# Three subtractions ahead of the multiplications in both normalizations of a post-norm transformer layer

## The chip, the cores and the metric

The kernel runs on one Trainium2 chip, on all 8 of its cores, as one program. The time is that of the device in microseconds, from start to end of the slowest core. No core talks to another: each computes 1024 token rows of the output.

## What is computed

```python
x = L0_attn_x                      # 4 x 2048 x 4096, float32
x = _layernorm(x + _L0_attn_ref(x, Wq, Wkv, Wo, bo))
x = _layernorm(x + _L0_ffn_ref(x, lora_A, lora_B, W, bias, lora_weights))

def _layernorm(x, axis=-1, eps=1e-5):
    m = jnp.mean(x, axis=axis, keepdims=True)
    v = jnp.var(x, axis=axis, keepdims=True)
    return (x - m) / jnp.sqrt(v + eps)
```

The attention has 32 heads of width 128 that share 8 groups of keys and values, with a causal mask. The second part is a product with a 4096 x 4096 matrix plus eight low-rank products of rank 16 that are summed.

## The kernel before, in words

A core holds its 1024 tokens along the free dimension; the 4096 features are 32 tiles of 128 partitions, indexed mc (or kc). So a tile of activations is 128 x 1024. The program is written engine by engine: each step appends a function to a list of its engine (em("v", ...) for VectorE, "t" TensorE, "c" ScalarE, "s" the SyncE queue, "g" the GpSimd queue), and each engine runs its list in the order written, with semaphores between them. There is no scheduler.

The stages are: keys and values for all tokens of the batch (L258, L269), queries (L336, L342), attention (L414 to L477), the division by the softmax sums (L526), the output projection with the first residual r1 (L585, L591, then L623/L625), which is stored to r1sc in DRAM, tile by tile, while two sums per token are collected on TensorE. f_v_fin1 makes mean and inverse deviation from the sums (L658 to L674); they go through DRAM (vec4) and come back broadcast to 128 partitions as bcm1 and bca1 (L682, L683).

**Stretch Y, the first normalization** (for mc in 0..31, f_v, L719 and L720): the tile r1[mc] is read back by SyncE (emit_r1rd, L542) into one of four slots, VectorE subtracts bcm1 into sb_y32 (L719) and multiplies that by bca1 into the bf16 tile ybf[mc] (L720). The helper vsync makes VectorE wait for the instruction it has just issued, and each tile waits for v_y of the one before. The read of tile mc, from 4 on, waits for v_y of tile mc-4. When all 32 are there, TensorE computes the low-rank product (f_t_h, L729, L735), then the big one (L765, L767); meanwhile r1 is read once more and normalized again, this time on VectorE with L794/L795, and the second residual r2 (L804, L806) is stored to r2sc (L824).

**Stretch O, the second normalization and the output**: after the second pair of sums (L830 to L846) SyncE loads the broadcast vectors bcm2 and bca2 (L854, L855) and the first four tiles of r2 (emit_r2rd, L870). Then per tile: VectorE subtracts (L886) and multiplies (L887) into one of two output buffers, SyncE stores it to the output (L892) and then reads tile mc+4. That order on SyncE is written as

```python
            def f_s2(sy, mc=mc):
                sy.wait_ge(SM["v_out"], mc + 1)
                sy.dma_start(out=d_out[mc], in_=vf32(OFF_OUTB[mc % 2], TOK)).then_inc(SM["so_out%d" % (mc % 2)], 16)
            em("s", f_s2)
            if mc + 4 < DC:
                emit_r2rd(mc + 4)
```

and is the same in both kernels. A subtraction waits for its read, for v_out of the tile before, and from tile 2 on for the store of tile mc-2 (so_out), which used the same output buffer.

Of the kernel before, what the change touches and what calls it, by code (L numbers as in the profile page):

```python
# [15 lines left out]
DC = 32  # L16
# [3 lines left out]
TOK = 1024  # L20
# [64 lines left out]
def build_nc():  # L85
# [38 lines left out]
    def sv(i):  # L124
        return arena[0:1, OFF_SV[i]:OFF_SV[i] + 4 * TOK].bitcast(F32)

    def ltmp(i):
        return arena[0:1, OFF_LTMP[i]:OFF_LTMP[i] + 4 * TOK].bitcast(F32)
    sb_r1bf = vbf(OFF_R1BF, TOK)
# [23 lines left out]
    def em(e, f):  # L153
        prog[e].append((cur_phase[0], f))
# [15 lines left out]
    with ExitStack() as es:  # L170
# [11 lines left out]
            "s_exp", "t_mmpc", "v_evl", "v_evctx", "v_norm", "v_nmul",  # L182
            "t_mmwo", "v_r1", "s_stats", "t_stats", "v_stat", "s_sqrt",
            "v_y", "t_mmh", "v_evh", "v_lbt", "t_mmf", "v_r2", "s_st2",
            "t_st2", "v_stat2", "s_sqrt2", "v_out", "v_seq",
        ]
        SM = {n: es.enter_context(nc.semaphore(n)) for n in semnames}

# [343 lines left out]
        def emit_r1rd(idx, extra_waits):  # L532
            slot = idx % 4
            r1rdc[slot] += 1
            tgt = 16 * r1rdc[slot]
            mc = idx % DC
            off = OFF_R1RD[slot]

            def f(sy, idx=idx, mc=mc, slot=slot, off=off, extra_waits=tuple(extra_waits)):
                for sn, val in extra_waits:  # L540
                    sy.wait_ge(SM[sn], val)
                sy.dma_start(out=vf32(off, TOK), in_=d_r1[mc]).then_inc(SM["sr1rd%d" % slot], 16)  # L542
            em("s", f)
            return tgt
# [159 lines left out]
        em("v", f_v_lbt)  # L704

        for mc in range(4, DC):
            r1rd_tgt[mc] = emit_r1rd(mc, [("v_y", mc - 3),
                                          ("ss_r1%d" % (mc % 2), 16 * (mc // 2 + 1))])
        for mc in range(DC):

            def f_v(v, mc=mc):
                slot = mc % 4
                v.wait_ge(SM["sr1rd%d" % slot], r1rd_tgt[mc])
                if mc == 0:
                    v.wait_ge(SM["s_bc"], 32)
                else:
                    v.wait_ge(SM["v_y"], mc)
                r1in = vf32(OFF_R1RD[slot], TOK)
                vsync(v, v.tensor_sub(sb_y32[:], r1in[:], sb_bcm1[:]))  # L719
                v.tensor_mul(sb_ybf[:, mc * TOK:(mc + 1) * TOK], sb_y32[:], sb_bca1[:]).then_inc(SM["v_y"], 1)  # L720
            em("v", f_v)

        def f_t_h(t):
            t.wait_ge(SM["s_lat"], 16)
# [24 lines left out]
        pending_stats2 = None  # L749
        for mc in range(DC):  # L750
            slot = mc % 2
            r1rd_tgt[DC + mc] = emit_r1rd(DC + mc, [("v_r2", mc - 3)] if mc >= 4 else [("v_y", DC)])

            def f_t(t, mc=mc, slot=slot):
                t.wait_ge(SM["gw%d" % slot], wt_tgt[mc])
                if mc == 0:
                    t.wait_ge(SM["v_evh"], 1)
                    t.wait_ge(SM["v_lbt"], 1)
                if mc >= 2:
                    t.wait_ge(SM["v_r2"], mc - 1)  # L760
                pair = P[mc % 2][:]
                wb = vbf(OFF_WBLK[slot], DC * 128)
                for kc in range(DC):
                    st = wb[:, kc * 128:(kc + 1) * 128]
                    t.matmul(pair[:, 0:512], st, sb_ybf[:, kc * TOK: kc * TOK + 512],  # L765
                             start=(kc == 0), stop=False)
                    t.matmul(pair[:, 512:1024], st, sb_ybf[:, kc * TOK + 512:(kc + 1) * TOK],  # L767
                             start=(kc == 0), stop=False)
                stl = sb_lbtb[:, mc * 128:(mc + 1) * 128]
                t.matmul(pair[:, 0:512], stl, sb_hb[:, 0:512], start=False, stop=True)  # L770
                t.matmul(pair[:, 512:1024], stl, sb_hb[:, 512:1024], start=False, stop=True).then_inc(SM["t_mmf"], 1)
            em("t", f_t)
            if pending_stats2 is not None:
                em("t", pending_stats2)

            def f_t_stats(t, mc=mc):
                t.wait_ge(SM["s_st2"], 2 * (mc + 1))
                if mc == 0:
                    t.wait_ge(SM["v_stat"], 2)
                t.matmul(P45[0:1, 0:512], sb_ones[:], sb_r1bf[:, 0:512],  # L780
                         start=(mc == 0), stop=(mc == DC - 1))
                t.matmul(P45[0:1, 512:1024], sb_ones[:], sb_r1bf[:, 512:1024],
                         start=(mc == 0), stop=(mc == DC - 1))
                t.matmul(P67[0:1, 0:512], sb_ones[:], sb_sqbf[:, 0:512],
                         start=(mc == 0), stop=(mc == DC - 1))
                t.matmul(P67[0:1, 512:1024], sb_ones[:], sb_sqbf[:, 512:1024],
                         start=(mc == 0), stop=(mc == DC - 1)).then_inc(SM["t_st2"], 1)

            def f_v(v, mc=mc, slot=slot):
                rslot = (DC + mc) % 4  # L790
                v.wait_ge(SM["sr1rd%d" % rslot], r1rd_tgt[DC + mc])
                if mc >= 1:
                    v.wait_ge(SM["v_r2"], mc)
                vsync(v, v.tensor_sub(sb_y32[:], vf32(OFF_R1RD[rslot], TOK)[:], sb_bcm1[:]))  # L794
                vsync(v, v.tensor_mul(sb_y32[:], sb_y32[:], sb_bca1[:]))  # L795
                v.wait_ge(SM["t_mmf"], mc + 1)
                if mc < 2:
                    v.wait_ge(SM["v_r1"], DC)
                if mc >= 2:
                    v.wait_ge(SM["ss_r2%d" % slot], 16 * (mc // 2))  # L800
                    v.wait_ge(SM["s_st2"], 2 * (mc - 1))
                pair = P[mc % 2][:]
                r2b = vf32(OFF_R2BUF[slot], TOK)
                v.scalar_tensor_tensor(r2b[:, 0:512], pair[:, 0:512], sb_bi[:, mc:mc + 1],  # L804
                                       sb_y32[:, 0:512], ALU.add, ALU.add)
                v.scalar_tensor_tensor(r2b[:, 512:1024], pair[:, 512:1024], sb_bi[:, mc:mc + 1],  # L806
                                       sb_y32[:, 512:1024], ALU.add, ALU.add).then_inc(SM["v_r2"], 1)
            em("v", f_v)

            def f_c(sc, mc=mc, slot=slot):  # L810
                sc.wait_ge(SM["v_r2"], mc + 1)
                if mc >= 1:
                    sc.wait_ge(SM["t_st2"], mc)
                if mc == 0:
                    sc.wait_ge(SM["t_stats"], DC)
                r2b = vf32(OFF_R2BUF[slot], TOK)
                sc.copy(sb_r1bf[:], r2b[:])  # L817
                sc.activation(sb_sqbf[:], r2b[:], AF.Square, bias=0.0, scale=1.0).then_inc(SM["s_st2"], 2)
            em("c", f_c)
            pending_stats2 = f_t_stats  # L820

            def f_s2(sy, mc=mc, slot=slot):
                sy.wait_ge(SM["v_r2"], mc + 1)
                sy.dma_start(out=d_r2[mc], in_=vf32(OFF_R2BUF[slot], TOK)).then_inc(SM["ss_r2%d" % slot], 16)  # L824
            em("s", f_s2)
# [35 lines left out]
        def emit_r2rd(mc):  # L861
            slot = mc % 4

            def f_s(sy, mc=mc, slot=slot):
                sy.wait_ge(SM["ss_r2%d" % (mc % 2)], 16 * (mc // 2 + 1))
                if slot >= 2 and mc < 4:
                    sy.wait_ge(SM["t_mmf"], DC)
                if mc >= 4:
                    sy.wait_ge(SM["v_out"], mc - 3)
                sy.dma_start(out=vf32(OFF_R2RD[slot], TOK), in_=d_r2[mc]).then_inc(SM["sr2rd%d" % slot], 16)  # L870
            em("s", f_s)

        for mc in range(4):
            emit_r2rd(mc)
        for mc in range(DC):
            slot = mc % 4

            def f_v(v, mc=mc, slot=slot):
                v.wait_ge(SM["sr2rd%d" % slot], r2rd_tgt6[mc])
                if mc == 0:  # L880
                    v.wait_ge(SM["s_bc"], 64)
                else:
                    v.wait_ge(SM["v_out"], mc)
                if mc >= 2:
                    v.wait_ge(SM["so_out%d" % (mc % 2)], 16 * (mc // 2))
                vsync(v, v.tensor_sub(sb_y32[:], vf32(OFF_R2RD[slot], TOK)[:], sb_bcm2[:]))  # L886
                v.tensor_mul(vf32(OFF_OUTB[mc % 2], TOK)[:], sb_y32[:], sb_bca2[:]).then_inc(SM["v_out"], 1)  # L887
            em("v", f_v)

            def f_s2(sy, mc=mc):  # L890
                sy.wait_ge(SM["v_out"], mc + 1)
# [4 lines that stand above are left out]
# [158 lines left out]
```

## Time and profile before

| what | us |
|---|---|
| median of 2 runs | 2995.86 |
| the runs | 2978.42 and 3013.3 |
| profiled execution, its own time | 2977.04 |
| its span on the slowest core (core 6) | 2975.4 |
| spans of the 8 cores | 2957.7 to 2975.4 |

The span is the time from the first to the last instruction of a core; the execution's own time lies 1.6 us above it. Rows of the trace are from core 6, in microseconds from the start of its span.

### The profile page before, as it was taken

Reading aid. Unit: us, or ns where it says so; the run is one execution under the profiler, and the core shown is the slowest. Engines: PE = TensorE matmul, PEld = TensorE weight load, DVE = VectorE, ACT = ScalarE, POOL = GpSimd, SP = SyncE. Lnnn points to the kernel's source line nnn. Section 1 sums busy time; section 2 is a strip of 40 time slices with the busy share of each in tenths; the row PEclk is TensorE's granted clock in tenths of the full one; section 3 lists DMA queues with packets and bytes.
Section 4 is the critical chain, followed back from the end, with each engine's and each line's share of the span. In section 5 each row is a group of like instructions: output and inputs, shape, how many; then the busy total and the mean of one; then the engine's idle time right before and its main releaser. Section 6 shows DMA issues by size and latency. Waiting matters only on the chain.

```text
span 2975.4 us, 32751 instructions; the slowest of 8 cores (2957.7 to 2975.4 us)
## 1 busy us (share of the span) xinstructions
PE 2441.4 (82%) x13257; PEld 1232.5 (41%) x13440; DVE 574.3 (19%) x662; ACT 551.8 (19%) x644; POOL 72.4 (2%) x140
## 2 busy tenths in 40 slices
PE   3888898899999878888988489999940799999900
PEld 3777787744444323333333134444410344444400
DVE  0110110100000001111111520000039222222256
ACT  0000000000000066677666111111110011111100
POOL 0000000000000000000000000000000000000000
PEclk9999998999999989999999689999975899999955
DMA  8878878544544410000000576666636455555558
GB/s 136 134 143 148 150 136 147 114 89 89 100 95 91 94 35 16 15 15 14 13 15 15 169 202 156 142 142 141 142 100 197 85 134 135 137 140 142 128 204 269
DMA packets 67129, 339.72 MB, mean 114 GB/s; under 512 B 8004, under 2 KB 8004, under 8 KB 49704
## 3 DMA queue, kind: packets, MB, share of 16 engines
q0 software_dynamic: 19584, 181.97, 35.1%
q1 hardware_dynamic: 47400, 155.65, 14.9%
q8 instruction: 111, 1.82, 0.2%
q14 instruction: 34, 0.28, 0.0%
HBM read 460.55 MB, written 59.00 MB: 175 GB/s over the span
## 4 chain that ended last, share of the span: by engine, by line
PE 75%; DMA 14%; DVE 8%; issue 2%; ACT 0%; DVEq 0%; SPq 0%; POOL 0%; POOLq 0%; ACTq 0%
PE P L767 8%; DMA arena<-xs 8%; PE P L342 7%; PE P L765 7%; PE P L591 7%; PE P L336 7%; PE P L585 7%; PE P L258 5%; PE P L269 5%; PE P L434 2%; PE P L443 2%; PE P L436 2%; DMA out<-arena 2%; PE P L448 2%; PE P L439 2%; PE P L445 2%
## 5 line engine op out<-in xcount | busy, mean ns | idle before, releaser
L477 ACT ACTIVATE arena<-P,arena 128x512 bf16<-128x512 f32 (+7 forms) x512 | 418.9, 830 | 183.9 <-PE P L414 145.8
L591 PE MATMUL P<-arena 128*128 128x512 bf16 x992 | 384.1, 387 | 24.6 <-DVE arena L526 21.4
L585 PE MATMUL P<-arena 128*128 128x512 bf16 x981 | 378.7, 386 | 21.3 <-DVE arena L526 21.3
L767 PE MATMUL P<-arena 128*128 128x512 bf16 x1024 | 389.3, 380 | 3.0 <-issue 1.0
L342 PE MATMUL P<-arena 128*128 128x512 bf16 x992 | 377.6, 381 | 12.1 <-DMA arena<-wq 10.0
L765 PE MATMUL P<-arena 128*128 128x512 bf16 x980 | 372.9, 381 | 11.5 <-DMA arena<-wt 11.5
L336 PE MATMUL P<-arena 128*128 128x512 bf16 x983 | 374.1, 381 | 0.0
L258 PE MATMUL P<-arena 128*128 128x256 bf16 x2048 | 247.0, 285 | 109.1 <-DMA arena<-xs 62.7
L258 PEld LDWEIGHTS P<-arena 128*128 128x128 bf16 x2048 | 207.5, 102 | 146.9 <-issue 114.7
L269 PE MATMUL P<-arena 128*128 128x256 bf16 x2048 | 228.8, 273 | 0.0
L269 PEld LDWEIGHTS P<-arena 128*128 128x128 bf16 x2048 | 200.4, 98 | 23.1
L477 ACT ACT_TABLE_LOAD x1 | 1.3, 1283 | 1050.0 <-PE P L414 1050.0
L585 PEld LDWEIGHTS P<-arena 128*128 128x128 bf16 x1024 | 100.4, 98 | 196.4 <-issue 83.2
L765 PEld LDWEIGHTS P<-arena 128*128 128x128 bf16 x1024 | 100.4, 98 | 143.1 <-issue 26.5
L336 PEld LDWEIGHTS P<-arena 128*128 128x128 bf16 x1024 | 100.6, 98 | 131.7 <-issue 11.8
L767 PEld LDWEIGHTS P<-arena 128*128 128x128 bf16 x1024 | 100.4, 98 | 117.9 <-issue 1.4
L342 PEld LDWEIGHTS P<-arena 128*128 128x128 bf16 x992 | 97.4, 98 | 117.9 <-issue 1.6
L463 DVE COPY arena<-P 1x1024 f32<-1x1024 f32 x32 | 38.8, 1212 | 548.0 <-PE P L448 548.0
L591 PEld LDWEIGHTS P<-arena 128*128 128x128 bf16 x992 | 97.3, 98 | 110.2 <-issue 0.5
L817 ACT CAST arena<-arena 128x1024 bf16<-128x1024 f32 x32 | 33.4, 1045 | 564.8 <-DVE arena L806 564.8
L434 PE MATMUL P<-arena 128*1 128x512 bf16 (+3 forms) x256 | 80.1, 313 | 52.1 <-DVE arena L464 52.1
L634 ACT CAST arena<-arena 128x1024 bf16<-128x1024 f32 x32 | 33.5, 1045 | 475.3 <-DVE arena L625 475.3
(107 smaller groups left out, 1966.4 us busy)
## 6 DMA issues: line engine op xcount, KB each, us to landing
arena<-xs POOLq DMA_DIRECT2D x32, 2048.0 KB, 16.2
arena<-wq POOLq DMA_DIRECT2D x32, 1024.0 KB, 8.4
arena<-wo POOLq DMA_DIRECT2D x32, 1024.0 KB, 10.4
arena<-r1sc SPq DMA_DIRECT2D x64, 512.0 KB, 4.9
arena<-wt POOLq DMA_DIRECT2D x32, 1024.0 KB, 8.9
arena<-linv SPq DMA_DIRECT2D x32, 512.0 KB, 5.7
arena<-xm SPq DMA_DIRECT2D x32, 512.0 KB, 10.4
r1sc<-arena SPq DMA_DIRECT2D x32, 512.0 KB, 9.7
```

What stands on the lines that cost most here:

```text
L258: mm = t.matmul(pair[:, 0:XTW], sb_wkv[:, kc * 512 + gl * 128: kc * 512 + gl * 128 + 128], xt[:, kc * XTW:(kc + 1) * XTW], start=(kc == 0) ...
L269: mm = t.matmul(pair[:, 0:256], xt[:, kc * XTW + s * 128: kc * XTW + s * 128 + 128], sb_wkv[:, kc * 512 + 256: kc * 512 + 512], start=(kc ...
L336: t.matmul(pair[:, 0:512], st, sb_xmbf[:, kc * TOK: kc * TOK + 512], start=(kc == 0), stop=(kc == DC - 1))
L342: t.matmul(pair[:, 512:1024], st, sb_xmbf[:, kc * TOK + 512:(kc + 1) * TOK], start=(kc == 0), stop=False)
L434: t.matmul(P67[0:1, s0:512], sb_ones[:], ex[:, s0:512], start=(kc == 0), stop=(kc == 7))
L436: t.matmul(P67[0:1, 512:1024], sb_ones[:], ex[:, 512:1024], start=(kc == 0), stop=(kc == KT - 1))
L439: t.matmul(P67[0:1, s0:1024], sb_ones[:], ex[:, s0:1024], start=False, stop=(kc == KT - 1))
L477: sc.activation(vbf(OFF_EXPS[Kg % 5], TOK)[:, s0:1024], pair[:, s0:1024], AF.Exp, bias=sb_consts[:, 0:1], scale=sb_consts[:, 1:2]).then_in ...
L585: t.matmul(pair[:, 0:512], st, sb_ctx[:, kc * TOK: kc * TOK + 512], start=(kc == 0), stop=(kc == DC - 1))
L591: t.matmul(pair[:, 512:1024], st, sb_ctx[:, kc * TOK + 512:(kc + 1) * TOK], start=(kc == 0), stop=False)
L765: t.matmul(pair[:, 0:512], st, sb_ybf[:, kc * TOK: kc * TOK + 512], start=(kc == 0), stop=False)
L767: t.matmul(pair[:, 512:1024], st, sb_ybf[:, kc * TOK + 512:(kc + 1) * TOK], start=(kc == 0), stop=False)
```

## The change

Both normalizations get six temporaries (ytmp) in place of the one sb_y32, and an order on VectorE in which the subtraction of tile mc stands ahead of the multiplication of tile mc-3. New semaphores v_ysub and v_osub count the subtractions; the reads into the four slots wait for them where they waited for v_y and v_out. In the second normalization the wait for the output buffer moves from the subtraction to the multiplication. The loop of L794/L795 stays as it is.

```diff
+    def ytmp(i):
+        return vf32(OFF_SV[i % 6], TOK)
...
         for mc in range(4, DC):
-            r1rd_tgt[mc] = emit_r1rd(mc, [("v_y", mc - 3),
+            r1rd_tgt[mc] = emit_r1rd(mc, [("v_ysub", mc - 3),
                                           ("ss_r1%d" % (mc % 2), 16 * (mc // 2 + 1))])
-        for mc in range(DC):
-
-            def f_v(v, mc=mc):
-                slot = mc % 4
-                v.wait_ge(SM["sr1rd%d" % slot], r1rd_tgt[mc])
-                if mc == 0:
-                    v.wait_ge(SM["s_bc"], 32)
-                else:
-                    v.wait_ge(SM["v_y"], mc)
-                r1in = vf32(OFF_R1RD[slot], TOK)
-                vsync(v, v.tensor_sub(sb_y32[:], r1in[:], sb_bcm1[:]))
-                v.tensor_mul(sb_ybf[:, mc * TOK:(mc + 1) * TOK], sb_y32[:], sb_bca1[:]).then_inc(SM["v_y"], 1)
-            em("v", f_v)
+        def yb_sub(v, mc):
+            slot = mc % 4
+            v.wait_ge(SM["sr1rd%d" % slot], r1rd_tgt[mc])
+            if mc == 0:
+                v.wait_ge(SM["s_bc"], 32)
+            if mc >= 6:
+                v.wait_ge(SM["v_y"], mc - 5)
+            v.tensor_sub(ytmp(mc)[:], vf32(OFF_R1RD[slot], TOK)[:], sb_bcm1[:]).then_inc(SM["v_ysub"], 1)
+
+        def yb_mul(v, mc):
+            v.wait_ge(SM["v_ysub"], mc + 1)
+            v.tensor_mul(sb_ybf[:, mc * TOK:(mc + 1) * TOK], ytmp(mc)[:], sb_bca1[:]).then_inc(SM["v_y"], 1)
+
+        def f_v_yb(v):
+            for mc in range(DC):
+                yb_sub(v, mc)
+                if mc >= 3:
+                    yb_mul(v, mc - 3)
+            for mc in range(DC - 3, DC):
+                yb_mul(v, mc)
+        em("v", f_v_yb)
...
-            r1rd_tgt[DC + mc] = emit_r1rd(DC + mc, [("v_r2", mc - 3)] if mc >= 4 else [("v_y", DC)])
+            r1rd_tgt[DC + mc] = emit_r1rd(DC + mc, [("v_r2", mc - 3)] if mc >= 4 else [("v_ysub", DC)])
...
                 if mc >= 4:
-                    sy.wait_ge(SM["v_out"], mc - 3)
+                    sy.wait_ge(SM["v_osub"], mc - 3)
                 sy.dma_start(out=vf32(OFF_R2RD[slot], TOK), in_=d_r2[mc]).then_inc(SM["sr2rd%d" % slot], 16)
...
+        def o_sub(v, mc):
+            slot = mc % 4
+            v.wait_ge(SM["sr2rd%d" % slot], r2rd_tgt6[mc])
+            if mc == 0:
+                v.wait_ge(SM["s_bc"], 64)
+            if mc >= 6:
+                v.wait_ge(SM["v_out"], mc - 5)
+            v.tensor_sub(ytmp(mc)[:], vf32(OFF_R2RD[slot], TOK)[:], sb_bcm2[:]).then_inc(SM["v_osub"], 1)
+
+        def o_mul(v, mc):
+            v.wait_ge(SM["v_osub"], mc + 1)
+            if mc >= 2:
+                v.wait_ge(SM["so_out%d" % (mc % 2)], 16 * (mc // 2))
+            v.tensor_mul(vf32(OFF_OUTB[mc % 2], TOK)[:], ytmp(mc)[:], sb_bca2[:]).then_inc(SM["v_out"], 1)
...
         for mc in range(DC):
-            slot = mc % 4
-
-            def f_v(v, mc=mc, slot=slot):
-                v.wait_ge(SM["sr2rd%d" % slot], r2rd_tgt6[mc])
-                if mc == 0:
-                    v.wait_ge(SM["s_bc"], 64)
-                else:
-                    v.wait_ge(SM["v_out"], mc)
-                if mc >= 2:
-                    v.wait_ge(SM["so_out%d" % (mc % 2)], 16 * (mc // 2))
-                vsync(v, v.tensor_sub(sb_y32[:], vf32(OFF_R2RD[slot], TOK)[:], sb_bcm2[:]))
-                v.tensor_mul(vf32(OFF_OUTB[mc % 2], TOK)[:], sb_y32[:], sb_bca2[:]).then_inc(SM["v_out"], 1)
-            em("v", f_v)
```

The function f_v6, not shown, calls o_sub and o_mul in the pattern of f_v_yb. Lines shift: in the changed kernel the subtraction and multiplication of stretch Y are L719 and L723, those of stretch O are L894 and L900, the read of r2 is L881 and the store of the output L915.

On VectorE, at the start of stretch O, stood before (tiles 0 to 3; sr2rd0 to 3 are the four read slots, so_out0 and 1 the two output buffers):

```order
L886 TENSOR_TENSOR arena<-arena 128x1024 [waits sr2rd0,s_bc]
L887 TENSOR_TENSOR arena<-arena 128x1024 [waits v_seq]
L886 TENSOR_TENSOR arena<-arena 128x1024 [waits sr2rd1,v_out]
L887 TENSOR_TENSOR arena<-arena 128x1024 [waits v_seq]
L886 TENSOR_TENSOR arena<-arena 128x1024 [waits sr2rd2,v_out,so_out0]
L887 TENSOR_TENSOR arena<-arena 128x1024 [waits v_seq]
```

and stands now:

```order
L894 TENSOR_TENSOR arena<-arena 128x1024 [waits sr2rd0,s_bc]
L894 TENSOR_TENSOR arena<-arena 128x1024 [waits sr2rd1]
L894 TENSOR_TENSOR arena<-arena 128x1024 [waits sr2rd2]
L894 TENSOR_TENSOR arena<-arena 128x1024 [waits sr2rd3]
L900 TENSOR_TENSOR arena<-arena 128x1024 [waits v_osub]
L894 TENSOR_TENSOR arena<-arena 128x1024 [waits sr2rd0]
L900 TENSOR_TENSOR arena<-arena 128x1024 [waits v_osub]
L894 TENSOR_TENSOR arena<-arena 128x1024 [waits sr2rd1]
```

The first multiplication moved behind the fourth subtraction, and the fifth subtraction, which needs the second load of slot 0, stands right behind it.

On the SyncE queue, at the same place, stands now (the first three rows are the last two of the four first reads and the store of tile 0, the fourth is the read of tile 4):

```order
L881 DMA arena<-r2sc 128x1024 [waits ss_r20,t_mmf]
L881 DMA arena<-r2sc 128x1024 [waits ss_r21,t_mmf]
L915 DMA out<-arena 128x1024 [waits v_out]
L881 DMA arena<-r2sc 128x1024 [waits ss_r20,v_osub]
L915 DMA out<-arena 128x1024 [waits v_out]
L881 DMA arena<-r2sc 128x1024 [waits ss_r21,v_osub]
```

Nothing moved here; only the wait of the reads from the fifth on has another name than before, where it was v_out.

## Rows read from the trace of the kernel before

**Rows 1.** The page's head: span, busy time per engine, TensorE's 40 slices.
```profile
span 2975.4 us, 32751 instructions; the slowest of 8 cores (2957.7 to 2975.4 us)
PE 2441.4 (82%) x13257; PEld 1232.5 (41%) x13440; DVE 574.3 (19%) x662; ACT 551.8 (19%) x644; POOL 72.4 (2%) x140
PE   3888898899999878888988489999940799999900
```
**Rows 2.** Table by stretches: PE, PEld, DVE, ACT, POOL; then clock, DMA share, GB/s.
```profile
2227.00:2312.00 85.00, 0.00 (x0) 0.00 (x0) 78.44 (x65) 0.00 (x0) 0.00 (x0) 0.50 0.55 173
2312.00:2340.00 28.00, 15.97 (x62) 6.73 (x64) 3.96 (x4) 0.00 (x0) 1.06 (x2) 0.80 0.36 66
...
2859.60:2975.40 115.80, 0.00 (x0) 0.00 (x0) 78.44 (x64) 0.00 (x0) 0.00 (x0) 0.50 0.84 282
```
**Rows 3.** Timeline, stretch Y: start, length, instruction (first, last, TensorE's next).
```profile
2227.43 1.22 DVE L719 TENSOR_TENSOR arena<-arena 128x1024 f32<-128x1024 f32 x1
...
2311.16 1.23 DVE L720 TENSOR_TENSOR arena<-arena 128x1024 bf16<-128x1024 f32 x1
...
2312.64 0.59 PE L729 MATMUL P<-arena 128*128 128x512 bf16 x1 [117.81 <-DVE arena L720]
```
**Rows 4.** Timeline, VectorE, behind the low-rank product.
```profile
2328.95 1.23 DVE L741 CAST arena<-P 128x1024 bf16<-128x1024 f32 x1 [16.57 <-PE P L732]
2330.09 1.22 DVE L794 TENSOR_TENSOR arena<-arena 128x1024 f32<-128x1024 f32 x1
2331.41 1.22 DVE L795 TENSOR_TENSOR arena<-arena 128x1024 f32<-128x1024 f32 x1
```
**Rows 5.** L542, the reads of r1sc, 2190 to 2320 us.
```profile
DMA to landing us min/median/max: 4.0/4.6/4.9
```
**Rows 6.** Waits in stretch O: who, for what, us in total, times, longest.
```profile
DVE arena L886 <- DMA out<-arena: 28.3, 26, 2.0
DVE arena L886 <- DMA arena<-r2sc: 8.6, 1, 8.6
```
**Rows 7.** Timeline, start of stretch O, VectorE and SyncE queue (SPq).
```profile
2853.51 2.31 SPq L870 DMA_DIRECT2D arena<-r2sc  x4
2859.60 1.23 DVE L886 TENSOR_TENSOR arena<-arena 128x1024 f32<-128x1024 f32 x1 [8.64 <-DMA arena<-r2sc]
2860.93 1.23 DVE L887 TENSOR_TENSOR arena<-arena 128x1024 f32<-128x1024 f32 x1
2862.23 0.34 SPq L892 DMA_DIRECT2D out<-arena  x1
...
2862.72 0.33 SPq L870 DMA_DIRECT2D arena<-r2sc  x1
...
2865.62 1.23 DVE L886 TENSOR_TENSOR arena<-arena 128x1024 f32<-128x1024 f32 x1 [0.81 <-DMA out<-arena]
```
**Rows 8.** Landings: stores L892, reads L870; then store 0, read 4, read 31, store 31.
```profile
DMA to landing us min/median/max: 2.6/4.3/5.4
DMA to landing us min/median/max: 4.5/6.2/9.0
out<-arena SPq DMA_DIRECT2D x1, 512.0 KB, 3.3
arena<-r2sc SPq DMA_DIRECT2D x1, 512.0 KB, 4.5
arena<-r2sc SPq DMA_DIRECT2D x1, 512.0 KB, 5.1
out<-arena SPq DMA_DIRECT2D x1, 512.0 KB, 2.6
```
**Rows 9.** Timeline, VectorE, end of stretch O: multiplications 28 and 31.
```profile
2961.03 1.23 DVE L887 TENSOR_TENSOR arena<-arena 128x1024 f32<-128x1024 f32 x1
...
2969.22 1.23 DVE L887 TENSOR_TENSOR arena<-arena 128x1024 f32<-128x1024 f32 x1
```
**Rows 10.** Table by stretches, the middle of stretch O, same columns as rows 2.
```profile
2862.00:2962.00 100.00, 0.00 (x0) 0.00 (x0) 68.53 (x57) 0.00 (x0) 0.00 (x0) 0.50 0.89 295
```

More of the change, by code:

```diff
@@ L184, in build_nc @@
             "v_y", "t_mmh", "v_evh", "v_lbt", "t_mmf", "v_r2", "s_st2",
-            "t_st2", "v_stat2", "s_sqrt2", "v_out", "v_seq",
+            "t_st2", "v_stat2", "s_sqrt2", "v_out", "v_seq", "v_ysub", "v_osub",
         ]
@@ L874, in build_nc, with f_v6 @@
             emit_r2rd(mc)
-        for mc in range(DC):
-            slot = mc % 4
-            def f_v(v, mc=mc, slot=slot):
-                v.wait_ge(SM["sr2rd%d" % slot], r2rd_tgt6[mc])
-                if mc == 0:
-                    v.wait_ge(SM["s_bc"], 64)
-                else:
-                    v.wait_ge(SM["v_out"], mc)
-                if mc >= 2:
-                    v.wait_ge(SM["so_out%d" % (mc % 2)], 16 * (mc // 2))
-                vsync(v, v.tensor_sub(sb_y32[:], vf32(OFF_R2RD[slot], TOK)[:], sb_bcm2[:]))
-                v.tensor_mul(vf32(OFF_OUTB[mc % 2], TOK)[:], sb_y32[:], sb_bca2[:]).then_inc(SM["v_out"], 1)
-            em("v", f_v)
+        def o_sub(v, mc):
[11 more added lines that the diff above has]
+            v.tensor_mul(vf32(OFF_OUTB[mc % 2], TOK)[:], ytmp(mc)[:], sb_bca2[:]).then_inc(SM["v_out"], 1)
+        def f_v6(v):
+            for mc in range(DC):
+                o_sub(v, mc)
+                if mc >= 3:
+                    o_mul(v, mc - 3)
+            for mc in range(DC - 3, DC):
+                o_mul(v, mc)
+        em("v", f_v6)
+        for mc in range(DC):
             def f_s2(sy, mc=mc):
```

## Prediction

> **What bounds the kernel now.** I read the page's head first [rows 1]: the core is busy on TensorE for 82% of 2975.4 us, and in its slices TensorE stands at 0 in two places late in the program, at slice 30 and in the last two slices. The table by stretches [rows 2] puts them at 2227 to 2312 us (the first normalization, "stretch Y") and 2859.6 to 2975.4 us (the last stage, "stretch O"). TensorE does nothing in either. All that the change edits lies in these two stretches, and both are on the path that sets the end, since TensorE waits for the last instruction of Y (117.8 us of idle time, released by L720) [rows 3] and nothing follows O.
>
> In Y, VectorE is the bound: 64 operations of 1.23 us, starting every 1.33 us without a break, from 2227.43 to 2312.39 us [rows 3]. The DMA engines are busy 0.55 of it [rows 2], and the reads of r1sc land in 4.0 to 4.9 us [rows 5], while four slots are in rotation.
>
> O is different. VectorE is busy 78.4 of 115.8 us, the DMA engines 0.84 [rows 2]. VectorE's waits say what is late: L886 (the subtraction) waited 26 times, 28.3 us in all, for out<-arena, the store that must free its output buffer; for a read only once, at the start [rows 6]. So reads arrive in time, and the two output buffers set the pace: multiplication 0 ends at 2862.16, multiplication 28 at 2962.26 us [rows 7, 9], 28 tiles in 100.1 us, 3.575 us each.
>
> **Edit 1, the waits on VectorE in stretch Y.** Instruction count stays 64. Removed are 32 waits on v_seq, each on the instruction just ahead, and 31 on v_y, likewise; the new order (three subtractions ahead) leaves only waits on results at least five instructions old, which are met before the engine comes to them. What a met wait costs is shown by a pair of the same length: L741 starts at 2328.95, lasts 1.23, and L794, which waits for nothing late, starts at 2330.09 us, 1.14 later; L794 to L795, with a v_seq wait between them, is 1.32 [rows 4]. So Y becomes 63 x 1.14 + 1.23 = 73.05 us, against 2312.39 - 2227.43 = 84.96 now: minus 11.9 us. Bounds: 0 (starts stay at 1.33 apart) and 11.9; I take 11.9, because the pair has the same engine and element count. Do the reads keep up? The read for tile n now starts when subtraction n-4 is done; there lie 8 x 1.14 - 1.23 = 7.9 us between that end and subtraction n, and read plus issue needs 0.13 + 4.9 + 0.10 = 5.1. On SP nothing else stands between these reads. The first one, tile 4, has only 5 x 1.14 - 1.23 = 4.5 us for 0.13 + 4.0 + 0.10 = 4.2. They just fit, so their cost is nothing; if landings grew past 7.6 us this cover would be gone and each microsecond would cost up to 28.
>
> The rows say 1.14 against 1.33 [rows 4]. The Trainium skill, "VectorE: DVE Perf Modes", section "The DRAIN you can't avoid", says that chaining operations without semaphores saves nothing (eight copies took 13.88 us either way). By that rule edit 1 would give 0; the trace speaks against it. It has a chance among the rivals below.
>
> **Edit 2, stretch O, is where I expect the loss.** The order on VectorE becomes sub 0, 1, 2, 3, mul 0, sub 4, mul 1, sub 5, and so on. The order on SP is unchanged: store n, then read n+4, store n+1, and so on. Read n+4 now waits for subtraction n (v_osub), which is early. But SP takes its instructions in order, and ahead of read n+4 stands store n, which waits for multiplication n. Multiplication n now comes after subtraction n+3, and the very next VectorE instruction is subtraction n+4, which waits for read n+4. So a read is issued only when VectorE is about to need it, where before it had four tiles' time. Behind the waiting subtraction stands multiplication n+1, behind that store n+1 on SP, and behind that read n+5. The loop is serial. Its pieces:
> - subtraction to multiplication start: 1.14 (no late wait between: store n-1 was issued a loop ago) [rows 4];
> - multiplication: 1.23 [rows 7];
> - its end (2860.93 + 1.23 = 2862.16) to the store's issue at 2862.23: 0.07 [rows 7];
> - store's issue to read's issue, 2862.23 to 2862.72: 0.49 [rows 7];
> - the read's landing, L;
> - landing to the subtraction's start: 0.10 (the store issued at 2862.23 landed in 3.3, at 2865.53, and L886 started at 2865.62) [rows 7, 8].
> Together 3.03 + L.
>
> L isn't shown in such a loop. Bounds: reads in Y, with nothing issued just ahead, 4.0 at least and 4.6 in the median [rows 5]; reads in O with almost 3.6 us of spacing and full DMA engines 6.2 in the median [rows 8]; and, below the reads, the stores at the end of the program, which have no read beside them, 2.6 [rows 8]. The nearest row is the first read of O's loop, 0.49 us behind a store just as it will be: 4.5 [rows 8]. The last loop read landed in 5.1 [rows 8]. I take 4.7, nearer the 4.5. One turn is then 7.73 us, against 3.575: 28 x 4.155 = +116.3 us.
>
> A sentence on what a page gives: the Trainium skill, "DMA: Bandwidth & Descriptors", section "Anatomy of one DMA — SWDGE (gpsimd) path", fits 2.0 us plus bytes over 436 GB/s, which for 512 KB is an estimate of 3.2 us, and by it the turn would be 6.2 us and the whole about 3040. The rows of reads here (4.0 to 4.9) lie above it, those of the last stores (2.6) below.
>
> The start of O: multiplication 0 now waits for subtraction 3, hence for read 3. That read is the last of four whose issues end at 2855.82, so it was issued at about 2855.5, and the longest landing in O is 9.0, so 2864.5 [rows 7, 8]. Then 0.10 + 1.14 + 1.23 makes 2866.97, 4.8 later than 2862.16; by VectorE alone it would be 2859.60 + 4 x 1.14 + 1.23 = 2865.39, 3.2 later. I take +4.0. The end: from the end of multiplication 28 to that of 31 it now takes 2970.45 - 2962.26 = 8.19 us [rows 9]; afterwards the subtractions are done, multiplication 30 waits for store 28 (0.07 + 2.6 + 0.10 after multiplication 28 [rows 8]), and 31 ends 1.14 + 1.23 later, 5.14 in all: -3.05. What follows multiplication 31 is the same.
>
> **Edit 3, the waits of the reads.** Reads 32 to 35 of r1sc wait for v_ysub instead of v_y, some 3 us sooner, into a time in which TensorE has the 16 us of L729 and L735 to do [rows 2]: nothing. The six temporaries lie on space used by vectors that have been stored by then: nothing.
>
> **The sum**, against the profiled execution, which took 2977.04 us around a span of 2975.4: 2977.04 - 11.9 + 116.3 + 4.0 - 3.05 = 3082.4, so 3082 us. The median shown, 2995.86, is of two runs, 2978.42 and 3013.3; the profiled execution lies by the lower one. Against 2978.42 the change is +3.5%.
>
> **Rivals.**
> 1. The reads stay ahead (not slower). If read n+4 went out on v_osub without standing behind store n, the output buffers would only hold back the multiplications: per two tiles 1.23 + 0.07 + 4.3 [rows 8] + 0.10 = 5.7 us, 2.85 a tile; but the two transfers of a tile, 1.05 MB, need 3.17 us at 295 / 0.89 = 331 GB/s [rows 10]. So 28 x (3.175 - 3.575) = -11 us in O, with Y -12: about 2954 us, -0.8%. For it: the diff loosens just this wait, and buffers are the cause of O's waits now. Against it: the order on SP, which has the store ahead of the read. It decides only if 3.03 + L is under 3.575, that is L under 0.55 us; no transfer of this size is near that.
> 2. Landings as short as the last stores': L = 2.6, a turn of 5.63, O 28 x 2.055 + 4.0 - 3.05 = +58.5, Y -11.9: 3024 us. For it: in the new loop one core moves 1.05 MB in some 7.7 us, 136 GB/s, far less than 295. Against it: reads in Y landed in no less than 4.0 at 173 GB/s. The Trainium skill's estimate of 3.2 us from "DMA: Bandwidth & Descriptors" falls in here.
> 3. Landings as long as now in O, because the store ahead occupies the same 16 engines: L = 6.2, a turn of 9.23, O 28 x 5.655 + 4.0 - 3.05 = +159.3, Y -11.9: 3124 us. Against it: rows 8's 4.5 behind a store.
> 4. The starts on VectorE stay 1.33 us apart with or without a late semaphore: Y gains nothing, and the turn has 1.33 instead of 1.14 in it: 3082.4 + 11.9 + 28 x 0.19 = 3100 us. For it: every one of the 63 steps in Y shows 1.33. Against it: the 1.14 in rows 4. This is what the rule of the Trainium skill in "VectorE: DVE Perf Modes", section "The DRAIN you can't avoid", would make of it.
>
> **How the numbers follow.** The serial loop with L between 4.0 (3063) and 5.1 (3094): 0.74. Rival 1: 0.04. Rival 2: 0.06. Rival 3: 0.09. Rival 4: 0.07. The low end, 3048, stands between rival 2 and L = 4.0; the high end, 3136, takes in rival 3 and its Y gain lost. A measurement of this kernel tells about 2% from no change, some 60 us. Rival 1 lies within that, and rival 2 partly. So slower 0.93, within 2% 0.06, faster 0.01.
>
> **What would show it.** Y: 64 starts 1.14 apart, about 73 us. O: VectorE's waits go to L894 <- DMA arena<-r2sc, 28 times some 5 us; waits for out<-arena nearly vanish; the chain alternates between reads of r2sc, L894 and L900; DMA share in O falls from 0.84 to about 0.4; O lasts some 233 us instead of 115.8. It is wrong if O's read waits are few (rival 1), or if O shows them but with another landing time (rivals 2, 3), or if starts in Y stay 1.33 apart (rival 4).

## The result, and the profile after

The changed kernel takes 3078.8 us in the median of 11 runs, the kernel before 2978.4 in 10: the ratio is 1.032, with a 95% interval of 1.029 to 1.036 (the two medians alone would give 1.034). Forecast were 3082 us and a loss of 3.5%. (Some runs were disturbed, with one half of the chip at a lower clock; the ratios and the single times given here and below leave them out, and the medians, which hold them, would be at most 1.2 us lower without.)

The head of the page of the profiled execution (3071.2 us, slowest core 2) shows the longer end: three slices of TensorE at 0 at the end where two were.

```profile
span 3069.7 us, 32924 instructions; the slowest of 8 cores (3052.1 to 3069.7 us)
PE 2457.1 (80%) x13440; PEld 1232.2 (40%) x13440; DVE 565.9 (18%) x662; ACT 551.4 (18%) x644; POOL 72.1 (2%) x140
PE   3888898899999788888886799999608999997000
```

The table by stretches, with the columns of [rows 2]: stretch Y, what lies between, and stretch O.

```profile
2230.90:2304.00 73.10, 0.00 (x0) 0.00 (x0) 72.85 (x65) 0.00 (x0) 0.00 (x0) 0.50 0.67 208
2850.40:3069.70 219.30, 0.00 (x0) 0.00 (x0) 75.67 (x64) 0.00 (x0) 0.00 (x0) 0.50 0.43 149
2304.00:2850.40 546.40, 508.39 (x2304) 219.36 (x2304) 138.09 (x137) 65.15 (x65) 16.89 (x32) 0.96 0.52 126
```

Y went from 84.96 to 73.0 us, O from 115.8 to 219.3, while its DMA share fell from 0.84 to 0.43. What lies between them is 546.4 against 547.2 before.

The timeline of VectorE in Y, its start and end, against [rows 3]:

```profile
2230.93 4.62 DVE L719 TENSOR_TENSOR arena<-arena 128x1024 f32<-128x1024 f32 x4
2235.47 1.22 DVE L723 TENSOR_TENSOR arena<-arena 128x1024 bf16<-128x1024 f32 x1
2236.61 1.22 DVE L719 TENSOR_TENSOR arena<-arena 128x1024 f32<-128x1024 f32 x1
2237.74 1.22 DVE L723 TENSOR_TENSOR arena<-arena 128x1024 bf16<-128x1024 f32 x1
2239.17 1.23 DVE L719 TENSOR_TENSOR arena<-arena 128x1024 f32<-128x1024 f32 x1 [0.21 <-DMA arena<-r1sc]
...
2299.35 4.61 DVE L723 TENSOR_TENSOR arena<-arena 128x1024 bf16<-128x1024 f32 x4
```

Starts are 1.14 apart but for one step of 1.43, before which the read of tile 5 came 0.21 us late. The end at 2299.35 + 4.61 = 2303.96 makes 73.03 us.

VectorE's waits in O, which answer to [rows 6]:

```profile
DVE arena L894 <- DMA arena<-r2sc: 145.1, 29, 8.4
DVE arena L900 <- DMA out<-arena: 1.8, 1, 1.8
```

The waits for a store are gone but for one, and 29 waits for a read stand in its place, five times as long in sum. The timeline shows one turn of the loop, against [rows 7]:

```profile
2862.00 1.22 DVE L894 TENSOR_TENSOR arena<-arena 128x1024 f32<-128x1024 f32 x1 [5.50 <-DMA arena<-r2sc]
2863.14 1.22 DVE L900 TENSOR_TENSOR arena<-arena 128x1024 f32<-128x1024 f32 x1
2864.44 0.34 SPq L915 DMA_DIRECT2D out<-arena  x1
2864.93 0.33 SPq L881 DMA_DIRECT2D arena<-r2sc  x1
2869.35 1.23 DVE L894 TENSOR_TENSOR arena<-arena 128x1024 f32<-128x1024 f32 x1 [4.99 <-DMA arena<-r2sc]
```

Subtraction, multiplication, store, read, and VectorE idle until the read has landed: one thing after another, although the subtraction belongs to a tile three ahead of the multiplication, and the read to one four ahead. The landings (the time from the issue of a transfer until it is complete) of the reads L881 and of the stores L915, which answer to [rows 8]:

```profile
DMA to landing us min/median/max: 3.8/4.1/7.7
DMA to landing us min/median/max: 2.6/2.9/3.8
```

### The profile page after: what moved, and what is told of

It is laid out like the page before. It is cut to its first block, busy times and chain, and to the rows that moved or that the text cites. A ratio compares the mean times of both kernels' runs of the same rounds, so it can differ in the third digit from the quotient of the medians.

```text
span 3069.7 us, 32924 instructions; the slowest of 8 cores (3052.1 to 3069.7 us)
## 1 busy us (share of the span) xinstructions
PE 2457.1 (80%) x13440; PEld 1232.2 (40%) x13440; DVE 565.9 (18%) x662; ACT 551.4 (18%) x644; POOL 72.1 (2%) x140
## 4 chain that ended last, share of the span: by engine, by line
PE 74%; DMA 15%; DVE 7%; issue 3%; SPq 0%; ACT 0%; DVEq 0%; POOL 0%; POOLq 0%; ACTq 0%
PE P L776 7%; PE P L339 7%; PE P L778 7%; PE P L588 7%; PE P L345 7%; PE P L594 7%; DMA arena<-xs 7%; PE P L261 6%; PE P L272 5%; DMA arena<-r2sc 4%; PE P L446 2%; PE P L437 2%; PE P L451 2%; PE P L439 2%; PE P L448 2%
## 5 line engine op out<-in xcount | busy, mean ns | idle before, releaser
L588 PE MATMUL P<-arena 128*128 128x512 bf16 x1024 | 396.3, 387 | 43.4 <-DVE arena L529 43.4
L776 PE MATMUL P<-arena 128*128 128x512 bf16 x1024 | 390.1, 381 | 11.0 <-DMA arena<-wt 11.0
L339 PE MATMUL P<-arena 128*128 128x512 bf16 x1024 | 389.6, 380 | 9.3 <-DMA arena<-wq 9.3
L778 PE MATMUL P<-arena 128*128 128x512 bf16 x1024 | 389.4, 380 | 0.0
L594 PE MATMUL P<-arena 128*128 128x512 bf16 x992 | 384.7, 388 | 0.0
L345 PE MATMUL P<-arena 128*128 128x512 bf16 x992 | 377.2, 380 | 0.0
L776 PEld LDWEIGHTS P<-arena 128*128 128x128 bf16 x1024 | 100.4, 98 | 142.9 <-issue 26.3
L339 PEld LDWEIGHTS P<-arena 128*128 128x128 bf16 x1024 | 100.4, 98 | 131.3 <-issue 11.0
L778 PEld LDWEIGHTS P<-arena 128*128 128x128 bf16 x1024 | 100.4, 98 | 117.9 <-issue 1.4
```

The lines of the kernel that those rows point to most:

```text
L339: t.matmul(pair[:, 0:512], st, sb_xmbf[:, kc * TOK: kc * TOK + 512], start=(kc == 0), stop=(kc == DC - 1))
L345: t.matmul(pair[:, 512:1024], st, sb_xmbf[:, kc * TOK + 512:(kc + 1) * TOK], start=(kc == 0), stop=False)
L588: t.matmul(pair[:, 0:512], st, sb_ctx[:, kc * TOK: kc * TOK + 512], start=(kc == 0), stop=(kc == DC - 1))
L594: t.matmul(pair[:, 512:1024], st, sb_ctx[:, kc * TOK + 512:(kc + 1) * TOK], start=(kc == 0), stop=False)
```

## The experiments

My theory: the new order on VectorE, together with the old order on SyncE, makes O serial, because each read stands behind a store that waits for a later multiplication; Y gains what the dropped waits on the instruction just ahead cost. Rivals: that the loss (or part of it) comes from Y, from the temporaries and the split itself, or from the number of slots and the read's own wait; and that a semaphore wait on VectorE costs nothing.

**Y alone.** O of the kernel before, Y of the changed one.

```diff
-                    sy.wait_ge(SM["v_osub"], mc - 3)
+                    sy.wait_ge(SM["v_out"], mc - 3)
...
-        em("v", f_v6)
...
+                vsync(v, v.tensor_sub(sb_y32[:], vf32(OFF_R2RD[slot], TOK)[:], sb_bcm2[:]))
+                v.tensor_mul(vf32(OFF_OUTB[mc % 2], TOK)[:], sb_y32[:], sb_bca2[:]).then_inc(SM["v_out"], 1)
+            em("v", f_v)
```

> Only stretch Y is changed (its order, its six temporaries, v_ysub); stretch O is as before. My theory, that Y gains by the met waits and that the loss is all in O: Y lasts 73 us, O 116, the whole 2966 us against 2978 before. The rival that a met semaphore is worth nothing by itself: 2978. The rival that part of the loss comes from Y (its reads late, or TensorE starting differently after a shorter pause): over 2978.

Measured: 2963.9 and 2972.7 us, beside 2974.6 to 2983.1 of the kernel before; forecast was 2966. Two runs are too few for an interval, and by their times alone the rival of no gain (2978) isn't far. The trace is clearer. Its timeline of Y:

```profile
2238.21 4.62 DVE L719 TENSOR_TENSOR arena<-arena 128x1024 f32<-128x1024 f32 x4
...
2306.34 4.62 DVE L723 TENSOR_TENSOR arena<-arena 128x1024 bf16<-128x1024 f32 x4
```

That is 72.75 us, and O lasts 2971.0 - 2857.7 = 113 us (116 forecast). So Y gains the 12 us, and no part of the loss is in it.

**O alone.** The reverse: Y as before, O changed.

```diff
-            r1rd_tgt[mc] = emit_r1rd(mc, [("v_ysub", mc - 3),
+            r1rd_tgt[mc] = emit_r1rd(mc, [("v_y", mc - 3),
...
-        em("v", f_v_yb)
...
+                vsync(v, v.tensor_sub(sb_y32[:], r1in[:], sb_bcm1[:]))
+                v.tensor_mul(sb_ybf[:, mc * TOK:(mc + 1) * TOK], sb_y32[:], sb_bca1[:]).then_inc(SM["v_y"], 1)
+            em("v", f_v)
```

> Only stretch O is changed, Y is as before (starts 1.33 apart, reads waiting for v_y). My theory, that the two parts add up: O 219 us, Y 85 us, the whole 3079 + 12 = 3091 us. If the parts don't add up, the time differs from 3091 by more than 5 us.

Measured: 3085.5 and 3100.5, median 3093.0, ratio 1.038 (1.033 to 1.043). Its Y lasts 84.96 us again, and VectorE's waits are those of the changed kernel (the subtraction of O is L886 in this version):

```profile
DVE arena L886 <- DMA arena<-r2sc: 147.0, 30, 8.8
```

The median is 2 us from the 3091 forecast, with two runs 15 us apart: the parts add up within what two runs can tell.

**Reads first on SyncE.** This is the test of the cause: nothing on VectorE differs.

```diff
+            for nx in ([4, 5, 6, 7] if mc == 0 else [mc + 7]):
+                if nx < DC:
+                    emit_r2rd(nx)
             em("s", f_s2)
-            if mc + 4 < DC:
-                emit_r2rd(mc + 4)
```

> The changed kernel with one edit: on SyncE, read n+7 is written ahead of store n (reads 4 to 7 ahead of store 0), so that no read stands behind a store that comes later than its own wait. Nothing on VectorE differs. My theory (order on the SyncE queue makes the loop serial): VectorE's read waits after the start vanish, a tile costs about 3.2 us, what the two transfers of 1.05 MB need at 331 GB/s, O lasts 105 to 108 us and the whole 2955 to 2960. The rival, that three subtractions ahead or the six temporaries cost the time by themselves (reads and stores colliding, VectorE held by the output buffers): over 3000 still.

Measured: 2963.4 us, ratio 0.9946 (0.9929 to 0.9963). The waits in O, and the table's row for its middle:

```profile
DVE arena L900 <- DMA out<-arena: 28.3, 23, 2.9
DVE arena L894 <- DMA arena<-r2sc: 12.3, 3, 11.7
```

```profile
2865.00:2940.00 75.00, 0.00 (x0) 0.00 (x0) 51.95 (x45) 0.00 (x0) 0.00 (x0) 0.50 0.91 314
```

The 145 us of read waits are 12.3, 11.7 of them the first. 115 us of the time are gone by moving DMAs on one queue. So the split, its temporaries and the three subtractions ahead are not what costs the time. The forecast of 2955 to 2960 was missed by 3 us. O lasts 2962.1 - 2852.0 = 110 us, 2 more than expected at most: at 314 GB/s a tile's 1.05 MB need 3.34 us, not 3.2, and the stores' landing is 5.5 us in the median in that middle, where it was 2.9 in the serial loop, so that the two output buffers hold back the multiplications again.

**Stores on ScalarE's queue.** The same repair by other means: order and waits stay, only the queue of the stores is another.

```diff
-            def f_s2(sy, mc=mc):
-                sy.wait_ge(SM["v_out"], mc + 1)
-                sy.dma_start(out=d_out[mc], in_=vf32(OFF_OUTB[mc % 2], TOK)).then_inc(SM["so_out%d" % (mc % 2)], 16)
-            em("s", f_s2)
+            def f_s2(sc, mc=mc):
+                sc.wait_ge(SM["v_out"], mc + 1)
+                sc.dma_start(out=d_out[mc], in_=vf32(OFF_OUTB[mc % 2], TOK)).then_inc(SM["so_out%d" % (mc % 2)], 16)
+            em("c", f_s2)
```

> The changed kernel with one edit: in O the 32 stores of the output are issued by ScalarE's queue, which has nothing else to do there, the reads stay on SyncE. The waits and VectorE's order are the same. My theory: read n+4 goes out when subtraction n is done, as the semaphore allows, the loop is no longer serial, and the time is that of the kernel with reads first, 2955 to 2960 us. The rival that the read's own wait or slot count is the limit: 3079 stays.

Measured: 2961.7 us, ratio 0.9945 (0.9928 to 0.9962), the same as with reads first, and 2 us above the forecast. Waits in O:

```profile
DVE arena L900 <- DMA out<-arena: 28.0, 21, 4.3
DVE arena L894 <- DMA arena<-r2sc: 12.0, 3, 11.1
```

Here the reads' wait is the loosened one of the change, v_osub of tile n-4, with four slots, and it does its work as soon as no store stands ahead.

**The loosened wait taken back.**

```diff
-                    sy.wait_ge(SM["v_osub"], mc - 3)
+                    sy.wait_ge(SM["v_out"], mc - 3)
```

> The changed kernel with one edit: reads 4 to 31 of r2 wait for v_out of tile n-4 (the multiplication), as before the change, not for v_osub. My theory: the store just ahead of each read on SyncE waits for that very multiplication, so the loosened wait never decides and nothing changes: 3079 us within 0.3%, turns of 7.2 us. The rival that the loosened wait buys something: slower than 3085.

Measured: 3075.0 us, in one run, inside the forecast of 3079 within 0.3%. Read waits:

```profile
DVE arena L894 <- DMA arena<-r2sc: 153.2, 30, 8.6
```

The reads of this run's slowest core are issued 7.5 us apart (3056.40 - 2853.12 over 27), not 7.2, because they landed in 4.5 in the median where they took 4.1 before; the other cores of this run show 3.9 to 4.5. The time is that of the changed kernel. So with this order on SyncE the wait that the diff loosens does not decide.

**Two subtractions ahead, and one.** The number that sets how far subtractions run ahead in O; SyncE's order untouched.

```diff
-                if mc >= 3:
-                    o_mul(v, mc - 3)
+                if mc >= 2:
+                    o_mul(v, mc - 2)
```

With one ahead the two numbers are 1.

> The changed kernel with one number changed: in O two subtractions stand ahead of the multiplication in place of three; Y and SyncE's order are untouched. Read n+4 is still written behind store n, but VectorE has subtraction n+3 and multiplication n+1 to do before it needs it, so one turn of 3.03 + L carries two tiles. With L of 5.5 to 6 at the higher load a tile costs 4.3 to 4.5 us, O 137 to 143, the whole 2986 to 2994 us. The rival that the distance doesn't matter, only that there is one at all (temporaries, their waits): near 3079.

Measured: 2982.1 us, ratio 1.0007 (0.9996 to 1.0019). The row for the middle of O, the landings of its reads, and the waits:

```profile
2875.00:2940.00 65.00, 0.00 (x0) 0.00 (x0) 36.72 (x32) 0.00 (x0) 0.00 (x0) 0.50 0.78 252
```

```profile
DMA to landing us min/median/max: 3.9/5.2/9.8
```

```profile
DVE arena L894 <- DMA arena<-r2sc: 59.6, 26, 10.6
```

The time is 4 us below the 2986 to 2994 forecast. The reads are issued 4.05 us apart (2964.93 - 2855.69 over 27), below the 4.3 to 4.5 I expected: I had put L at 5.5 to 6, and it is 5.2. With it (3.03 + 5.2) / 2 = 4.1. A turn carries two tiles, and the whole kernel is back at the time of before: what Y wins, O loses.

> The same with one subtraction ahead in O: a turn of 3.03 + L carries three tiles, so with L = 6.2 it would allow 3.1 us a tile, less than the 3.34 that the transfers need at the 314 GB/s seen with reads first. My theory: no read waits but at the start, the DMA engines bound O (share 0.9), and with SyncE's order untouched the time is that of the kernel with reads first, 2960 to 2964 us. The rival that the reads must be moved on SyncE to gain: over 2975.

Measured: 2959.3 us, ratio 0.9933 (0.9916 to 0.995), the time of reads first (the intervals overlap) without touching SyncE. The row, the waits, and the landings of its reads:

```profile
2875.00:2940.00 65.00, 0.00 (x0) 0.00 (x0) 45.94 (x40) 0.00 (x0) 0.00 (x0) 0.50 0.95 323
```

```profile
DVE arena L894 <- DMA arena<-r2sc: 28.6, 17, 10.5
DVE arena L900 <- DMA out<-arena: 5.0, 8, 1.0
```

```profile
DMA to landing us min/median/max: 4.7/6.4/9.3
```

The read waits after the first sum to 18 us, so they are not gone as I had said; but the DMA engines are 0.95 busy, so I take these for waits on transfers in progress. Tiles per turn are 4 minus the number of subtractions ahead: 7.2 us a tile with three ahead, 4.05 with two, 3.2 with one (read issues, (2948.76 - 2861.91) / 27). The last is close to (3.03 + 6.4) / 3 = 3.14, so the turn and the DMA engines set about the same pace there, and this run does not tell which of them holds it.

**What a read's landing is made of.** The loop without the stores of tiles 0 to 27, and so without the waits for their output buffers. It leaves those tiles out of the result and serves only to read the loop.

```diff
-                    sy.wait_ge(SM["v_osub"], mc - 3)
+                    sy.wait_ge(SM["v_out"], mc - 3)
...
-            em("s", f_s2)
+            if mc >= 28:
+                em("s", f_s2)
```

> Measures what a read's landing is made of in the serial loop. The changed kernel without the output stores of tiles 0 to 27 (those results never reach the output), the reads waiting for v_out so that the loop stays serial. The read is then alone in the loop. A turn should be 1.14 + 1.23 + 0.07 + L + 0.10 = 2.54 + L. If the store that goes out 0.49 us ahead is what a read waits behind, L falls from 4.1 to about 3.1 and a turn to 5.6 us. If a read alone takes 4.0, as the shortest of stretch Y before, L stays and a turn is 6.6.

The numbers are of core 1, and of the trace alone; the reads of all eight cores land in 3.2 to 3.3 us in the median. Landings of its reads, and the starts of two turns of VectorE, one after the other:

```profile
DMA to landing us min/median/max: 3.1/3.2/7.9
```

```profile
2994.59 1.23 DVE L894 TENSOR_TENSOR arena<-arena 128x1024 f32<-128x1024 f32 x1 [3.46 <-DMA arena<-r2sc]
...
3000.59 1.23 DVE L894 TENSOR_TENSOR arena<-arena 128x1024 f32<-128x1024 f32 x1 [3.64 <-DMA arena<-r2sc]
```

A read of 512 KB with nothing else of its core in flight lands in 3.2 us, and from subtraction 4 to 31 a turn takes 5.83 ((3012.51 - 2855.00) / 27), near the 5.6 forecast. The stores are worth 0.9 us of the landing, and 0.49 by their issue. That the 0.9 is the core's own store 0.49 us ahead is argued, not shown: the stores of the other seven cores are gone in this version too.

**What bounds O once it is not serial.** Reads first with four output buffers in place of two:

```diff
-OFF_OUTB = (16384, 20480)
+OFF_OUTB = (131072, 135168, 139264, 143360)
...
-            if mc >= 2:
-                v.wait_ge(SM["so_out%d" % (mc % 2)], 16 * (mc // 2))
+            if mc >= 4:
+                v.wait_ge(SM["so_out%d" % (mc % 4)], 16 * (mc // 4))
```

> The kernel with reads first, with four output buffers in place of two (in the space of ybf, which is free in O). It tells whether output buffers or the DMA engines bound O there. If the DMA engines do, as 0.91 busy and 314 GB/s say, VectorE's 28 us of waits for stores turn into waits for reads and the time stays at 2962 within 0.2%. If the buffers do, a tile falls towards VectorE's 2.3 us and the whole to 2935 to 2945 us.

Measured: 2956.9 us, ratio 0.9921 (0.9897 to 0.9945). The row for the middle of O, VectorE's waits, and the landings of the reads and of the stores:

```profile
2875.00:2940.00 65.00, 0.00 (x0) 0.00 (x0) 50.34 (x43) 0.00 (x0) 0.00 (x0) 0.50 1.01 344
```

```profile
DVE arena L894 <- DMA arena<-r2sc: 23.2, 19, 10.8
DVE arena L900 <- DMA out<-arena: 6.9, 14, 1.1
```

```profile
DMA to landing us min/median/max: 6.7/10.9/12.4
DMA to landing us min/median/max: 3.6/10.8/12.6
```

The waits for stores fell from 28.3 to 6.9 us, and those for reads rose by as little as 10.9, to 23.2. The time, 5 us under 2962, lies at the lower edge of the 0.2% that I had given, 6.5 under what two buffers measured, and far from the 2935 to 2945 of a kernel held by buffers alone. The share of the DMA engines is 1.01 at 344 GB/s, and now every transfer stands in line: a store lands in 10.8 us where it took 5.0 with reads first and two buffers. They are the floor here.

Then the kernel before with the four output buffers and no reordering:

```diff
-OFF_OUTB = (16384, 20480)
+OFF_OUTB = (131072, 135168, 139264, 143360)
...
-                if mc >= 2:
-                    v.wait_ge(SM["so_out%d" % (mc % 2)], 16 * (mc // 2))
+                if mc >= 4:
+                    v.wait_ge(SM["so_out%d" % (mc % 4)], 16 * (mc // 4))
```

> The kernel before, with four output buffers in stretch O in place of two and nothing else: no reordering anywhere. My theory, that O before was held by the two output buffers and next by the DMA engines: VectorE's 28 us of waits for stores go, a tile costs 3.05 to 3.1 us (1.05 MB at 344 GB/s) in place of 3.575, O falls by 12 to 14 us, the whole to 2964 to 2967. The rival that splitting subtraction and multiplication is needed for O's gain: 2978.

Measured: 2967.9 us, ratio 0.9956 (0.9939 to 0.9972).

```profile
DVE arena L886 <- DMA arena<-r2sc: 25.8, 16, 11.4
```

```profile
2875.00:2940.00 65.00, 0.00 (x0) 0.00 (x0) 48.30 (x41) 0.00 (x0) 0.00 (x0) 0.50 1.00 320
```

The time is 1 us above the forecast. No wait for a store is left (the one line shown is the wait for reads, which land in 9.4 us in the median and the stores in 8.0), and O lasts 2966.4 - 2862.1 = 104.3 us, 11.5 less than before. So O can gain by more buffers, without any split of subtraction and multiplication.

Last, one subtraction ahead with four output buffers.

> The changed kernel with one subtraction ahead in O and four output buffers, SyncE's order untouched. O is bound by the DMA engines either way, so the same as reads first with four buffers: 2953 to 2958 us. If reads still come late because each stands behind a store, 2959 to 2962.

Measured: 2956.6 us, ratio 0.9918 (0.9901 to 0.9936), and all four runs lie between 2956.3 and 2958.0.

```profile
2875.00:2940.00 65.00, 0.00 (x0) 0.00 (x0) 47.91 (x41) 0.00 (x0) 0.00 (x0) 0.50 1.01 326
```

This and reads first with four buffers have the lowest times, 0.8% under the kernel before and 4% under the changed one. But the two more buffers are worth little on top of one subtraction ahead: 2.7 us in the medians, with overlapping intervals, and O itself is no shorter, 105.6 against 105.4 us on the slowest cores.

## Why the prediction was right

**Edit 1, Y.** Forecast 73.05 us and a gain of 11.9; measured 73.03. The price of a met wait, 1.14 us from start to start, came from one pair of rows and held for 62 of the 63 steps. (The nearest result that an instruction waits for is four instructions old, not five, at the start and the end of the stretch; starts are 1.14 apart there too.) Rival 4 is out; the rule of the Trainium skill in "VectorE: DVE Perf Modes", section "The DRAIN you can't avoid", that chaining without semaphores saves nothing, doesn't hold for a wait on the instruction just ahead: 1.33 with it, 1.14 without. The reads kept up as worked out but for one: the tight one was that of tile 5, not 4, since the landings grew to 5.9 us at most, where 4.9 was the longest before; it cost 0.2 us.

**Edit 2, O.** The mechanism, a read behind a store behind a later multiplication, is what the timeline shows, and reads first and stores on ScalarE's queue, which take it away in two independent ways, each bring back some 115 us. Each piece of the turn outside L held: 1.14, 1.22, 0.08, 0.49 and about 0.1. The one term that was mis-sized is L: 4.7 taken, 4.1 in the median, 4.2 on average (7.24 - 3.03). From the end of multiplication 0 to that of 28 it took 3059.30 - 2856.50 = 202.8 us, 7.24 a tile against my 7.73, so the term is +102.7 and not +116.3. My value leaned on two reads that each had another read still in flight beside them; in the run without stores the 4.1 become 3.2, so the stores are worth 0.9. The start of O cost +3.5 (taken 4.0), the end -2.9 (taken -3.05), what follows the last multiplication +0.1.

**The sum.** 102.7 + 3.5 - 2.9 + 0.1 - 11.9 = +91.5 us in the two stretches. The spans differ by 3069.7 - 2975.4 = 94.3; of the rest, 3.5 lie ahead of Y and -0.8 between Y and O, on different cores of different executions, whose spans differ by 18 us within one. Over the medians the difference is 100.4, the forecast was +105.4. So the 13.6 us by which L's term was too large are partly made up in the comparison of times by what the sum did not hold, the spread between cores and runs (the profiled execution after, 3071.2, is at the low end of 3071.2 to 3083.9). That 3082 came within 4 us of the median is in that part luck: the mechanism was right, and L was 0.5 to 0.6 us too long.

**Edit 3.** No sign of it, as forecast.

**Rivals.** Rival 1, reads that stay ahead, was put at 2954 and needed the store out of the way; with it out of the way the kernel takes 2962 to 2963, where the row shows 314 GB/s and not 331 with two buffers, and 2957 with four. Rival 2 (L = 2.6) and rival 3 (6.2) lie on both sides of 4.1. The Trainium skill's fit in "DMA: Bandwidth & Descriptors", section "Anatomy of one DMA — SWDGE (gpsimd) path", is for the GpSimd queue and gives an estimate of 3.2 us for 512 KB; these reads, on SyncE's queue, took just that without stores. It has no term for other transfers in flight, with which they took 4.1.

## What to carry to other kernels

A queue issues in the order written, so a prefetch is as early as the latest wait written ahead of it. When compute is reordered so that its producer runs k tiles ahead of its consumer, every load that is written behind the consumer's store loses k tiles of its lead; look for the pair "store n, load n+slots" and move the load k places up, or put stores and loads on two queues. And ask first what holds the loop. In O it was two output buffers, with the DMA engines next at 0.9 busy. O took 114 us before (in the median of the eight cores, from the first subtraction to the end), 104 with two more output buffers and no split, 106 with one subtraction ahead and no more buffers, 107 with both, and 100 with reads first and four buffers. So either repair alone comes near the bound of the DMA engines; three subtractions ahead with the old order on SyncE threw that away. The 12 us of Y, where VectorE itself was the bound, came from the split alone.

## What the runs showed of the hardware that I had not expected

The landing of a 512 KB read ran from 3.2 us, with no store in flight, over 4.1 in the serial loop and 5.2 at 252 GB/s to 10.9 at 344 GB/s. That is why the turn was shorter than I took it: a serial loop lowers its own load and so its landings. The rate alone doesn't set the landing, though: it was 6.4 at 323 GB/s (one subtraction ahead, two output buffers) and 9.4 at 320 GB/s (the order of before, four output buffers). What differs there is how many transfers stand in line. An estimate of it, read landing plus store landing over the time in which a tile's 1.05 MB move, is 1.0 in the serial loop, 3.5 and 5.3 in these two (store landings 4.9 and 8.0 us), and 7.1 in the run with 10.9. That this number sets the landing is my reading, not tested by itself.

The share of the DMA engines was 0.91 at 314 GB/s with reads first and two output buffers, and 1.01 at 344 GB/s with four: the engines had idle time with two. But a share of 1.00 to 1.01 went with 320 and 326 GB/s in the other two versions with four output buffers, so a full share isn't one rate. What sets the rate there these runs don't show.
